# Attention's row sums: a DMA and GpSimd fold three accumulators into one before TensorE sums it

## What is computed

```python
h = _ada_ln(x, cond, Wln1, bln1)
x = x + _attn(h, Wq, bq, Wk, bk, Wv, bv, Wo, bo)
# in _attn, L = 2048, 16 heads of 32:
scores = jnp.einsum('bhqd,bhkd->bhqk', q, k) / np.sqrt(HD).astype(x.dtype)
attn = jax.nn.softmax(scores, axis=-1)
out = jnp.einsum('bhqk,bhkd->bhqd', attn, v)
```

## Time and profile before

| what | value |
|---|---|
| runs | 3097.61 us median of 3 (3094.74 to 3099.68) |
| the profiled execution | 3095.97 us, its span 3094.5 us |
| granted TensorE clock over the span | 0.995 |
| the attention stage | from about 350 to 1900 us of the span |
| line 853, accumulating DMAs | 189, 1024 KB each, 8.5 us to landing in the median |
| line 861, additions of GpSimd | 217, mean 4587 ns |
| line 866, merges of GpSimd | 31, mean 4607 ns |
| line 689, products with ones | 528 instructions, 62.6 us |

### The profile page before, as it was taken

One profiled execution on the slowest core, in us unless ns is written; L12 is line 12 of the kernel. 1 busy time (PEld: TensorE's weight loads), 2 busy tenths in 40 slices (PEclk: granted clock), 3 DMA queues, 4 the chain that ended last, 5 costly groups with the idle time before them and its releaser, 6 DMA issues.

```text
span 3094.5 us, 42984 instructions
## 1 busy us (share of the span) xinstructions
PE 3063.0 (99%) x16138; PEld 2134.4 (69%) x16138; DVE 2157.8 (70%) x3633; ACT 1389.2 (45%) x2703; POOL 1546.5 (50%) x655
## 2 busy tenths in 40 slices
PE   8999999999999999999999999999999999999999
PEld 7887655555555555555555545788888888788998
DVE  4457888999989999899898978643333333246776
ACT  2221466666666666666666674321111111023332
POOL 0000289898898988988989884300000000102222
PEclk9999999999999999999999999999999999999999
DMA  6675688879788798887977767720111110321221
GB/s 208 187 221 160 169 169 174 186 150 199 169 175 186 149 199 169 171 190 148 201 168 166 171 148 224 244 83 1 41 41 41 41 41 16 109 69 63 79 87 58
DMA packets 169366, 423.39 MB, mean 137 GB/s; under 512 B 18493, under 2 KB 60605, under 8 KB 141864
## 3 DMA queue, kind: packets, MB, share of 16 engines
q0 software_dynamic: 27744, 201.08, 32.1%
q1 hardware_dynamic: 139639, 214.07, 23.0%
q10 hardware_dynamic: 1776, 5.51, 0.7%
HBM read 143.51 MB, written 75.50 MB: 71 GB/s over the span
## 4 chain that ended last, share of the span: by engine, by line
PE 94%; DVE 2%; DMA 2%; POOL 1%; issue 1%; ACT 0%; SPq 0%; DVEq 0%; ACTq 0%; POOLq 0%
PE ps L384 16%; PE ps L672 15%; PE ps L683 15%; PE ps L1207 11%; PE ps L1194 11%; PE ps L460 5%; PE ps L1756 4%; PE ps L464 3%; PE ps L1773 3%; PE ps L689 2%; PE ps L1794 1%; PE ps L1549 1%; PE ps L158 1%; DMA x<-in_x 1%; PE ps L293 1%
## 5 line engine op out<-in xcount | busy, mean ns | idle before, releaser
L397 DVE TENSOR_REDUCE nmp<-ps 128x1 f32<-128x512 f32 x1966 | 1199.3, 679 | 108.9 <-PE ps L384 104.3
L762 ACT ACTIVATE pt<-ps 128x512 f32<-128x512 f32 x2048 | 1030.9, 625 | 459.4 <-PE ps L672 456.2
L861 POOL TENSOR_TENSOR pt<-pt 128x2048 f32<-128x2048 f32 x217 | 995.3, 4587 | 119.7 <-ACT pt L762 115.0
L672 PE MATMUL ps<-qs,ks 128*128 128x512 f32 x2048 | 810.8, 400 | 2.5 <-ACT pt L762 2.5
L384 PE MATMUL ps<-ks,qs 96*128 96x512 f32 x1966 | 803.6, 409 | 0.1
L384 PEld LDWEIGHTS ps<-ks,qs 96*128 96x128 f32 x1966 | 372.6, 190 | 265.5 <-DVE nmp L397 167.3
L683 PE MATMUL ps<-pt,vq 128*32 128x512 f32 x4096 | 493.7, 600 | 0.0
L672 PEld LDWEIGHTS ps<-qs,ks 128*128 128x128 f32 x2048 | 389.3, 191 | 96.4 <-ACT pt L762 17.9
L1207 PE MATMUL ps<-w,gp 128*128 128x512 f32 x1536 | 379.1, 395 | 1.8 <-DVE gp L1323 1.8
L1194 PE MATMUL ps<-hpb,w 128*128 128x512 f32 x1536 | 379.0, 396 | 0.0
L1207 PEld LDWEIGHTS ps<-w,gp 128*128 128x128 f32 x1536 | 288.2, 188 | 71.0 <-DVE gp L1323 2.6
(11 more groups left out here) (169 smaller groups left out, 2869.2 us busy)
## 6 DMA issues: line engine op xcount, KB each, us to landing
pt<-pt POOLq DMA_DIRECT2D x189, 1024.0 KB, 8.5
qk_d<-st SPq DMA_DIRECT2D x128, 256.0 KB, 2.9
qs<-qk_d SPq DMA_DIRECT2D x87, 256.0 KB, 4.8
ks<-qk_d SPq DMA_DIRECT2D x42, 512.0 KB, 8.5
xina<-in_x SPq DMA_DIRECT2D x8, 1024.0 KB, 6.4
v_d<-vst SPq DMA_DIRECT2D x32, 256.0 KB, 2.7
vq<-v_d SPq DMA_DIRECT2D x32, 256.0 KB, 4.2
ao_d<-accs SPq DMA_DIRECT2D x32, 256.0 KB, 7.4
```

Of the source, the lines that this page charges most:

```text
L397: dve.tensor_reduce(nmp[:, n // 4, n % 4:n % 4 + 1], ps[:, ring.bank["max", u], :], AX.X, ALU.max, negate=True).then_inc(s_mr, 1)
L672: pe.matmul(ps[:, score_bank(n), :], ksb[w % 2][:, hh, 128 * kt:128 * kt + 128], qsb[:, v % 3, hh, :], start=True, stop=True).then_inc(s_s ...
L762: act.activation(pt[:, exp_slot(g), hh, :], ps[:, score_bank(n), :], ACT.Exp, scale=SCALE).then_inc(s_exp, 1)
L861: pool.tensor_tensor(accumulator(v, 0), accumulator(v, 0), pt[:, exp_slot(g), :, :], ALU.add).then_inc(s_add, 1)
```

## The change

- The DMA lists become (3, 7, 12) and (5, 10, 14), GpSimd's list (4, 6, 8, 9, 11, 13, 15).
- In units 0 to 29, behind tile 15's addition, GpSimd waits for both accumulators' DMAs and issues a seventh DMA that adds accumulator 1 onto accumulator 2. In the next unit, at tile 3 and behind that tile's DMA, GpSimd waits for the seventh DMA and adds accumulator 2 onto accumulator 0 (`pool_merge`).
- TensorE multiplies only accumulator 0 by ones in these units, and does so in phase 4 of the next unit; VectorE's copy moves to phase 5. Units 30 and 31 keep two or more accumulators and phase 2 (unit 30 merges at its tile 15).
- `dma_count` counts the seventh DMA in.

```diff
--- before.py
+++ after.py
@@ -34,8 +34,8 @@
 EARLY = 84
 ACCS = 3
 RING = 6
-ADD_DMA = ((3, 7, 11), (5, 9, 13))
-ADD_POOL = (4, 6, 8, 10, 12, 14, 15)
+ADD_DMA = ((3, 7, 12), (5, 10, 14))
+ADD_POOL = (4, 6, 8, 9, 11, 13, 15)
 LAST_DMA = ((5, 10), (6,))
 LAST_DVE = (3, 4, 7, 8, 9, 11, 12, 13, 14)
 LAST_PE = (15,)
@@ -63,7 +63,13 @@
 
 def dma_count(v, d, kt):
 
-    return 16 * (len(ADD_DMA[d]) * v + dma_tiles(v, d).index(kt) + 1)
+
+    return 16 * (len(ADD_DMA[d]) * v + d * min(v, NU - 2) + dma_tiles(v, d).index(kt) + 1)
+
+
+def sums_phase(v):
+
+    return 4 if v < NU - 2 else 2
 
 
 def add_count(v, kt):
@@ -101,7 +107,7 @@
             for i in range(8):
                 if EARLY - 2 + 8 * p + i < 64 * NU:
                     self.use(("max", EARLY - 2 + 8 * p + i))
-            if f == 2 and v:
+            if v and f == sums_phase(v - 1):
                 self.use(("sums", v - 1))
         self.use(("sums", NU - 1))
 
@@ -694,6 +700,7 @@
 
         def pe_sums(v):
 
+
             bank = ring.bank["sums", v]
             last = v == NU - 1
             pe_bank_free(("sums", v))
@@ -703,10 +710,11 @@
                     pe_ones(bank, pt[:, exp_slot(16 * v + kt), :, :], kt == LAST_PE[0], False)
                 pe.wait_ge(s_dma[1], dma_count(v, 1, dma_tiles(v, 1)[-1]))
                 pe_ones(bank, accumulator(v, 2), False, False)
-            pe.wait_ge(s_dma[0], dma_count(v, 0, dma_tiles(v, 0)[-1]))
-            pe_ones(bank, accumulator(v, 1), not last, False)
+            if v >= NU - 2:
+                pe.wait_ge(s_dma[0], dma_count(v, 0, dma_tiles(v, 0)[-1]))
+                pe_ones(bank, accumulator(v, 1), not last, False)
             pe.wait_ge(s_add, add_count(v, added_tiles(v)[-1]) + (0 if last else 1))
-            pe_ones(bank, accumulator(v, 0), False, True).then_inc(s_end, 1)
+            pe_ones(bank, accumulator(v, 0), v < NU - 2, True).then_inc(s_end, 1)
 
         def pe_attention():
             pe.wait_ge(s_mr, EARLY - 2)
@@ -812,7 +820,7 @@
                 if v == NU - 1 and f in (0, 2):
                     dve_split_wo(f)
                     dve_split_wo(f + 1)
-                if f == 3 and v:
+                if v and f == sums_phase(v - 1) + 1:
                     dve_sums(v - 1)
                 for i in range(8):
                     u = EARLY - 2 + 8 * p + i
@@ -835,6 +843,13 @@
             pool.wait_ge(s_rec, 4 * v + 4)
             pool.wait_ge(s_accv, v + 1)
             pool.tensor_tensor(accs[:, v % 2, :], accv[:, v % 2, :], accs[:, v % 2, :], ALU.mult).then_inc(s_an, 1)
+
+        def pool_merge(v):
+
+            whole = dma_count(v, 1, dma_tiles(v, 1)[-1]) + (16 if v < NU - 2 else 0)
+            pool.wait_ge(s_dma[1], whole)
+            pool.wait_ge(s_add, add_count(v, added_tiles(v)[-1]))
+            pool.tensor_tensor(accumulator(v, 0), accumulator(v, 0), accumulator(v, 2), ALU.add).then_inc(s_add, 1)
 
         def pool_attention():
             pool.memset(ones[:, :], 1.0).then_inc(s_on, 1)
@@ -860,10 +875,14 @@
                         pool.wait_ge(s_add, add_count(v, kt) - 1)
                     pool.tensor_tensor(accumulator(v, 0), accumulator(v, 0), pt[:, exp_slot(g), :, :],
                                        ALU.add).then_inc(s_add, 1)
-                if v < NU - 1 and kt == 15:
+                if v < NU - 2 and kt == 15:
+                    pool.wait_ge(s_dma[0], dma_count(v, 0, dma_tiles(v, 0)[-1]))
                     pool.wait_ge(s_dma[1], dma_count(v, 1, dma_tiles(v, 1)[-1]))
-                    pool.wait_ge(s_add, add_count(v, 15))
-                    pool.tensor_tensor(accumulator(v, 0), accumulator(v, 0), accumulator(v, 2), ALU.add).then_inc(s_add, 1)
+                    pool.dma_start(accumulator(v, 2), accumulator(v, 1), accum_op=ALU.add).then_inc(s_dma[1], 16)
+                if v == NU - 2 and kt == 15:
+                    pool_merge(v)
+                if 0 < v < NU - 1 and kt == 3:
+                    pool_merge(v - 1)
                 if kt == 5 and v >= 2:
                     pool_values(v - 2)
                 if kt == 10 and v == NU - 1:
```

## The result

The changed kernel takes 3326.51 us (median of 4 runs, 3321.22 to 3330.11), the kernel before beside it 3098.49 us: a ratio of 1.0738, 95% interval 1.0724 to 1.0752. It is 228 us slower, where 176 us (3274) was forecast and 3335 was the upper end of the range. The profiled execution's span is 3324.5 us, 230 us over the one before.

What follows compares the result with a forecast made beforehand. GpSimd's ring of 36.1 + 7.9 + 9.85 + 0.1 = 54.0 us was to set the unit, against 48.13 before; 30 x 5.87 = 176 us more gave 3274 us beside the median, range 3190 to 3335.

Steps and rivals of the forecast that it cites:

- What bounds the kernel: Before the change TensorE, 99% busy, paces attention at 48.13 us a unit; after it GpSimd's 54.0 us wins over TensorE's 47.8.
- the ring: GpSimd's in-order chain from one merge to the next, with two DMA landings in it: 54.0 us a unit.
- Merge to DMA 14: GpSimd's additions, merge, DMA issues and product, from the merge to the issue of tile 14's DMA: 36.1 us.
- The seventh's landing: Time until the seventh DMA has landed, sized by tile 3's DMA as its nearest row: 9.85 us.
- DMA 14's landing: Time until tile 14's accumulating DMA has landed, sized by tile 11's and tile 13's DMAs: 7.9 us.
- The two steps from a landing to what waits for it: On GpSimd, what waits for a DMA starts at once when it has landed: two such steps, 0.1 us.
- Part 1: TensorE sums one accumulator of two in units 0 to 29: 0.855 us a unit removed, 30 x 0.855 = 25.7 us.
- Part 2: Sums to phase 4, copy to 5: VectorE's late phase 3 start costs 0.5 us with signals, leaving 0.35 of 0.855.
- A: Rival: GpSimd's ring stays hidden and TensorE sets the unit; 10 us gained, 3087 us, down to 3072; chance 5%.
- B: Rival: the ring is there, but both landings take only 7.0 to 7.6 us; 50.8 us a unit, 3179 us; chance 7%.
- C: Rival: ring forecast holds and TensorE's slower clock after pauses adds 30 x 1.5 = 45 us, 3319 us; chance 10%.
- The unit count and the slack: Units 1 to 30 each pay 5.87 us, 176 us; slack between GpSimd and the buffers is used up once, early.

## Why the prediction was right, and where its size was off

**What bounds the kernel, and the ring.** Right. GpSimd's ring of waits sets the unit: its length accounts for all 228 us, halving the seventh shortens it one to one, and the merge behind tile 6 gives 165 us back.

**The terms of the ring.** Merge to DMA 14: 36.1 forecast, 36.12 in the mean of 29 units. That it fits so well is part luck: addition 8, with another addition behind it, takes 5.28 us from start to start, not 4.74, and the merge (4.54) and the product (1.25) take 0.20 and 0.25 less than their terms. The seventh's landing: 9.85 forecast, 9.80. DMA 14's landing: 7.9 forecast, 9.20; this is the term that was mis-sized most. The two steps from a landing to what waits for it: 0.1 together forecast, from one merge's start; the merge's is 0.08, but the issue of the seventh starts 0.54 behind DMA 14's landing in every unit. 1.30 and 0.52 us, 30 times, are 55 us; the gap between 176 and 228 us is 52. As for DMA 14, I took tile 11's and tile 13's DMAs as its nearest rows, and they were so by what they carry, not by when: in the changed kernel DMA 14 is issued when the next unit has begun, and flies where that unit loads its keys. Where the next unit loads keys it is 10.6 and 11.5 us from its issue to the seventh, elsewhere 8.5 and 8.6. Tile 3's DMA, 9.9 us in the earlier trace rows, had the nearer place in time.

**Part 1.** Right: 0.855 us forecast, 0.87 by the sums' phase in the run with one sum in phase 2, of which VectorE takes back 0.14; 288 instructions in the sums' line. In the changed kernel it is worth nothing, since TensorE sets no unit's length there.

**Part 2.** Right in kind: 0.5 us a unit forecast, 0.40 read from phase 3; 0.35 of the 0.855 were to be left, 0.47 are, by the units without accumulator 1. In the changed kernel it too is hidden. That the end of attention is untouched was wrong: the sums of unit 30 wait for its later merge, 5.4 us once.

**What to see in the profile.** The merge's wait and the wait for DMA 14 came as forecast (3.8 us in the mean of 27 waits for DMA 14, where 3 was said). The exponentials of tiles 11 and 13 wait for DMAs, as forecast, 88.3 and 30.5 us over all units; those of tile 9 do too, 45.3 us, for DMA 3, which the forecast did not see. "TensorE waits for VectorE in phase 3 by no more than 0.5" held.

**Rivals.** A (hidden ring) and B (short landings) are out: no landing of the seventh is under 7.0, its median 9.7. C, the clock: its 3319 us lie nearer to the 3326.51 than the 3274 of the forecast, but not for its reason. The clock does fall. TensorE in the changed kernel, at a pause, and two stretches (us, busy by engine, then the granted clock, DMA share, GB/s):

```profile
1091.28 0.50 PE L678 MATMUL ps<-qs,ks 128*128 128x512 f32 x1 [2.46 <-ACT pt L770]
1091.70 2.69 PE L689 MATMUL ps<-pt,vq 128*32 128x512 f32 x16
```

```profile
1091.30:1096.00 4.70, 4.70 (x25) 1.00 (x25) 0.00 (x0) 1.39 (x3) 4.70 (x3) 0.65 0.00 0
1096.00:1102.50 6.50, 3.87 (x20) 2.83 (x16) 5.79 (x10) 2.75 (x6) 6.50 (x4) 0.99 1.02 209
```

After 2.46 us without an exponential the values take 2.69 us instead of 1.92, at a granted clock of 0.65, part of the stretch at 1.2 GHz. But 30 x 7.60 is all there is, and the ring has no TensorE time in it (merge to DMA 14 is 36.0 to 36.4 us in every unit but the first): the clock's price vanished in the time that TensorE had to spare, as the forecast had it.

**The unit count and the slack.** 30 units at the full excess held: the first merge waits already, at 411.72.

## What to carry to other kernels

When a change puts a wait for a transfer on an in-order queue, follow that queue round to the same wait in the next turn and add it up: some 43 us of GpSimd's own work with two landings in its way were 56 us, and it, not TensorE, set the pace. Size each landing by the rows at the time of the turn at which it will fly, not by the rows of the same kind. Where a transfer is moved off the waiting queue, look next at what it now delays in the DMA queue: the seventh cost tile 3's transfer 4 us from one place and its own 5 us from another.

## What the runs showed of the hardware

Accumulating transfers of 1 MB in a queue hold each other up: issued directly behind another, the seventh lands after 14.1 us in the median (11.4 to 18.3), and after 9.1 (6.9 to 11.3) where it is issued by itself, between two additions. A half-size one, 512 KB, lands after 6.7 us instead of 9.7: half of the bytes save some 3 us, under a third of the landing. A DMA issue of GpSimd that waits for a landing starts 0.54 us behind it, an addition 0.08 us. Additions of GpSimd with a DMA issue behind them kept their 4.5 us from start to start in the changed kernel too, with a transfer more on the way; addition 8, ahead of addition 9, took 5.28 us, where the first of two in a row took 4.74 in the kernel before.
